# Weight checks loaded one output tile ahead, W2 casts spread over the first block, and three of seven W1 quadrants read without a copy

## What is computed

```python
tf = sigmoid(sum(cond, -1)); decay = exp(-exp(w)) * (0.5 + 0.5 * tf)
ek = exp(min(fside, 30)); ekv = ek * fside
# forward and backward scans over the 1024 time steps: a = a * decay + ekv_t ; b = b * decay + ek_t
num = nf + nb - ekv + exp(u + fside) * fside ; den = df + db - ek + exp(u + fside)
mixed = sigmoid(x) * num / max(den, 1e-8) * (0.8 + 0.2 * tf)
h = mixed @ W1.T                       # 1024 -> 4096
a = gelu(clip(round(h / 0.1)) * 0.1)
out = x + a @ W2.T                     # 4096 -> 1024
```

## Time and profile before

| | |
|---|---|
| median of 3 runs | 1911.16 us (1910.56 to 1913.1) |
| the profiled execution | 1906.45 us |
| its span in the profile | 1904.6 us |
| TensorE matmul busy | 1723.3 us, 90% |
| VectorE busy | 1281.7 us, 67% |
| ScalarE busy | 1046.7 us, 55% |
| last output matmul of block 0, 1, 7 ends at | 356.7, 576.9, 1897.6 us |

### The profile page before, as it was taken

One profiled execution on the slowest core, in us unless ns is written; L12 is line 12 of the kernel. 1 busy time (PEld: TensorE's weight loads), 2 busy tenths in 40 slices (PEclk: granted clock), 3 DMA queues, 4 the chain that ended last, 5 costly groups with the idle time before them and its releaser, 6 DMA issues.

```text
span 1904.6 us, 27493 instructions
## 1 busy us (share of the span) xinstructions
PE 1723.3 (90%) x10882; PEld 1076.1 (57%) x10882; DVE 1281.7 (67%) x2040; ACT 1046.7 (55%) x1422; POOL 24.7 (1%) x44
## 2 busy tenths in 40 slices
PE   1367989899998999899998999989998999989998
PEld 0123434487446864388545874478544884468643
DVE  8964987679586766678685775768776774933211
ACT  5544853488336863388444873378544883345400
POOL 0040000000000000000000000000000000000000
PEclk9678999899998999999998999989998999999999
DMA  8499866465454645456454654556454554545442
GB/s 215 116 238 334 299 204 182 144 198 191 148 168 143 188 150 177 144 181 213 139 174 136 199 170 142 171 169 194 153 183 132 178 189 148 157 132 161 142 146 73
DMA packets 119990, 329.55 MB, mean 173 GB/s; under 512 B 13232, under 2 KB 21424, under 8 KB 119344
## 3 DMA queue, kind: packets, MB, share of 16 engines
q1 hardware_dynamic: 117168, 304.67, 50.5%
q0 software_dynamic: 2688, 23.07, 5.1%
HBM read 319.30 MB, written 48.23 MB: 193 GB/s over the span
## 4 chain that ended last, share of the span: by engine, by line
PE 79%; DMA 3%; DVE 3%; ACT 1%; issue 1%; SPq 0%; DVEq 0%
PE ps L561 42%; PE ps L505 37%; DMA chk_full<-in_w_dram 3%; DVE chk_full L1107 1%; ACT chk_i L758 1%; DVE a L1039 0%; ACT mo L695 0%; DVE a L1041 0%; DVE a L1043 0%; DVE xy L1099 0%; SPq L303 0%; SPq L317 0%; DVE mo L1049 0%; SPq L318 0%; ACT q L699 0%
## 5 line engine op out<-in xcount | busy, mean ns | idle before, releaser
L561 PE MATMUL ps<-act,w_ring 128*128 128x512 f16 x4096 | 890.1, 379 | 9.4 <-DVE xy L1099 9.4
L505 PE MATMUL ps<-mo,w_ring 128*128 128x256 f16 x6272 | 704.4, 276 | 61.2 <-DVE mo L1049 59.6
L505 PEld LDWEIGHTS ps<-mo,w_ring 128*128 128x128 f16 x6272 | 620.5, 99 | 146.7 <-DVE mo L1049 61.6
L561 PEld LDWEIGHTS ps<-act,w_ring 128*128 128x128 f16 x4096 | 400.6, 98 | 490.9 <-issue 15.5
L758 ACT ACTIVATE chk_i<-chk_full 128x1024 int8<-128x1024 f32 x64 | 67.5, 1054 | 440.3 <-DMA chk_full<-in_w_dram 440.3
L1107 DVE SCALAR_TENSOR_TENSOR chk_full<-chk_i,chk_full 128x1024 f32<-128x1024 int8 x64 | 78.3, 1223 | 252.5 <-ACT chk_i L758 252.3
L1092 DVE SCALAR_TENSOR_TENSOR act<-a,act 128x1024 f16<-128x1024 f32 x128 | 156.2, 1220 | 132.3 <-ACT act L751 132.3
L745 ACT ACTIVATE a<-q 128x1024 f32<-128x1024 int16 x128 | 135.3, 1057 | 31.4 <-DVE act L1092 27.2
L751 ACT ACTIVATE act<-a 128x1024 f16<-128x1024 f32 x128 | 134.2, 1049 | 0.9
L482 PE MATMUL ps<-mo,w_ring 128*128 128x512 f16 x128 | 45.1, 532 | 87.3 <-DVE mo L1032 87.3
L495 PE MATMUL ps<-mo,w_ring 128*128 128x512 f16 x384 | 90.0, 399 | 16.5 <-ACT q L699 12.5
(11 more groups left out here) (95 smaller groups left out, 1454.2 us busy)
## 6 DMA issues: line engine op xcount, KB each, us to landing
w_ring<-w1s SPq DMA_DIRECT2D x168, 512.0 KB, 3.7
w_ring<-w_half SPq DMA_DIRECT2D x144, 512.0 KB, 4.2
chk_full<-in_w_dram SPq DMA_DIRECT2D x64, 512.0 KB, 5.2
V<-in_fside_dram SPq DMA_DIRECT2D x64, 256.0 KB, 4.5
R<-in_x_dram SPq DMA_DIRECT2D x64, 256.0 KB, 4.6
w_half<-in_w_dram POOLq DMA_DIRECT2D x16, 1024.0 KB, 14.5
xy<-in_x_dram SPq DMA_DIRECT2D x64, 256.0 KB, 2.6
out_dram<-xy SPq DMA_DIRECT2D x64, 256.0 KB, 4.4
```

The source lines that it names most:

```text
L505: mm = pe.matmul(dst[:, f, :], wp_ring[:, k, r, f, q, :], mo[:, op, q, p, :], start=(fresh and f == 0 and q == 0 and p == 0), stop=(q == K ...
L561: mm = pe.matmul(y_ps[y][:, :], w2_ring[:, k, f, :], act[:, a, p, :], start=(a == 0 and p == 0), stop=(a == FT - 1 and p == 1))
```

## The change

1. `load_check` moves ahead by one output tile: pieces 1 and 2 are asked for before the loop over d, and iteration d asks for piece d + 1. The wait inside it stays. One ring load moves between the two.
2. The hand-written order of DVE and ACT in the output stage is changed: the operands of group 0 and 1, parts of mixing tiles and the division of tile 7 now stand ahead of checks they stood behind.
3. The eight W2 casts no longer follow the W1 casts at once. Each waits on GpSimd for a point of the work: the seventh mixed tile, the first hidden steps, later hidden steps, the first outputs. The ring loads of W2 wait for the cast they need, not for all.
4. The 24 copies of plain W1 quadrants are gone. `w1s` holds the four sums only. The plain quadrants are read from `w1_half`, as two runs of 1 KB for each partition; a chunk of a plain and a summed quadrant is now loaded by two DMAs on one semaphore.

```diff
-        w1s = nc.dram_tensor("w1s", [STEPS, P, 7, 2, KH * P], F16).ap()
+        w1s = nc.dram_tensor("w1s", [STEPS, P, 4, 2, KH * P], F16).ap()
...
-                        yield flat[:, 0:2 * PROD], 2 * PROD, s_p5, g + 1
+                        yield [(0, PROD, w1_quads[s][:, 0, :, 0, :]), (PROD, PROD, flat[:, 0:PROD])], s_p5, g + 1
                         if s > 0:
-                            yield prev[:, 2 * PROD:4 * PROD], 2 * PROD, s_p3, g
-                        yield flat[:, 4 * PROD:6 * PROD], 2 * PROD, s_p6, g + 1
+                            prev = w1s[s - 1].rearrange("p r f q -> p (r f q)")
+                            yield [(0, 2 * PROD, prev[:, PROD:3 * PROD])], s_p3, g
+                        yield [(0, PROD, flat[:, 3 * PROD:4 * PROD]), (PROD, PROD, w1_quads[s][:, 0, :, 1, :])], s_p6, g + 1
                         if s > 0:
-                            yield prev[:, 6 * PROD:7 * PROD], PROD, s_p4, g
+                            yield [(0, PROD, w1_quads[s - 1][:, 1, :, 1, :])], s_p4, g
...
-                if i == 2 * STEPS:
-                    for d in range(DT):
-                        sp.wait_ge(s_w2cast[d], 16)
+                if 2 * STEPS <= i < 2 * STEPS + 4:
+                    sp.wait_ge(s_w2cast[i % 2], 16)
+                if 2 * STEPS + 4 <= i < 2 * STEPS + 2 * DT:
+                    sp.wait_ge(s_w2cast[(i - 2 * STEPS) // 2], 16)
...
-                for _ in range(3 if n == 0 else 5):
+                for _ in range(2 if n == 0 else 4):
                     ring_load()
                 load_check(DT * n + 1)
+                ring_load()
+                load_check(DT * n + 2)
                 for d in range(2, DT):
...
-                    load_check(DT * n + d)
+                    if d < DT - 1:
+                        load_check(DT * n + d + 1)
...
             for d in range(DT):
+                if d == 0:
+                    pool.wait_ge(s_out, CT - 1)
+                elif d == 1:
+                    pool.wait_ge(s_h0, 2 * FPS)
+                elif d < 6:
+                    pool.wait_ge(s_h0, FPS * (d + 3))
+                else:
+                    pool.wait_ge(s_y, d - 5)
                 pool.dma_start(w2_half[d], w2_full[d]).then_inc(s_w2cast[d], 16)
-            for s in range(STEPS):
-                pool.wait_ge(s_w1cast[s], 16)
-                for r, h, k in ((WP1, 0, 0), (WP2, 0, 1), (WP4, 1, 1)):
-                    pool.dma_start(w1s[s][:, r, :, :], w1_quads[s][:, h, :, k, :]).then_inc(s_w1copy, 16)
```

More of the change, by code:

```diff
@@ L262, in ring_chunks @@
                 w2_part = [[w2_half[d].rearrange("p (h n) -> p h n", h=2)[:, h, :] for h in range(2)] for d in range(DT)]
-                yield w2_part[0][0], SLOT, s_y, y_half(n, 0, 0)
+                yield [(0, SLOT, w2_part[0][0])], s_y, y_half(n, 0, 0)
                 if n > 0:
-                    yield last[:, 2 * PROD:4 * PROD], 2 * PROD, s_p3, g + 1
-                yield w2_part[1][0], SLOT, s_y, y_half(n, 1, 0)
+                    yield [(0, 2 * PROD, last[:, PROD:3 * PROD])], s_p3, g + 1
+                yield [(0, SLOT, w2_part[1][0])], s_y, y_half(n, 1, 0)
                 if n > 0:
-                    yield last[:, 6 * PROD:7 * PROD], PROD, s_p4, g + 1
-                yield w2_part[0][1], SLOT, s_y, y_half(n, 0, 1)
-                yield w2_part[1][1], SLOT, s_y, y_half(n, 1, 1)
+                    yield [(0, PROD, w1_quads[LAST][:, 1, :, 1, :])], s_p4, g + 1
+                yield [(0, SLOT, w2_part[0][1])], s_y, y_half(n, 0, 1)
+                yield [(0, SLOT, w2_part[1][1])], s_y, y_half(n, 1, 1)
                 for d in range(2, DT):
                     for h in range(2):
-                        yield w2_part[d][h], SLOT, s_y, y_half(n, d, h)
+                        yield [(0, SLOT, w2_part[d][h])], s_y, y_half(n, d, h)
         block = ctx.enter_context(nc.Block())
@@ L300, in ring_load @@
                 if i >= RING:
-                    sp.wait_ge(*chunks[i - RING][2:])
-                src, size = chunks[i][:2]
-                sp.dma_start(w_ring[:, i % RING, 0:size], src).then_inc(s_ring[i % RING], 16)
+                    sp.wait_ge(*chunks[i - RING][1:])
+                for place, size, src in chunks[i][0]:
+                    dst = w_ring[:, i % RING, place:place + size]
+                    if len(src.shape) == 3:
+                        dst = dst.rearrange("p (f q) -> p f q", f=2)
+                    sp.dma_start(dst, src).then_inc(s_ring[i % RING], 16)
             def load_prefix(g):
@@ L466, in _ @@
             used = [0]
+            pieces = [len(chunk[0]) for chunk in ring_chunks()]
             def loaded():
@@ L470, in loaded @@
                 used[0] = i + 1
-                pe.wait_ge(s_ring[i % RING], 16 * (i // RING + 1))
+                pe.wait_ge(s_ring[i % RING], 16 * sum(pieces[i % RING:i + 1:RING]))
                 return i % RING
@@ L840, in _ @@
                     reciprocal(g0 + 7)
-                check_i8(at + 7)
+                check_i8(at + 6)
                 if nxt:
                     operands_hi(n + 1, 3)
+                check_i8(at + 7)
             def general_block(m):
@@ L1180, in _ @@
                     operands_lo(n + 1, 0)
+                check(at)
                 residual_sum(n, 0)
-                check(at + 1)
+                if nxt:
+                    part(3, g0 + 4)
                 residual_sum(n, 1)
                 if nxt:
-                    part(3, g0 + 4)
                     part(0, g0 + 5)
-                check(at + 2)
+                check(at + 1)
                 if nxt:
@@ L1190, in _ @@
                     operands_lo(n + 1, 1)
+                    part(1, g0 + 5)
                 residual_sum(n, 2)
+                check(at + 2)
                 if nxt:
-                    part(1, g0 + 5)
                     part(2, g0 + 5)
                     part(3, g0 + 5)
-                check(at + 3)
                 residual_sum(n, 3)
@@ L1199, in _ @@
                     part(0, g0 + 6)
+                check(at + 3)
+                if nxt:
                     part(1, g0 + 6)
                     part(2, g0 + 6)
-                check(at + 4)
                 residual_sum(n, 4)
@@ L1206, in _ @@
                     part(0, g0 + 7)
+                check(at + 4)
+                if nxt:
                     part(1, g0 + 7)
-                check(at + 5)
                 residual_sum(n, 5)
@@ L1212, in _ @@
                     part(3, g0 + 7)
-                check(at + 6)
+                check(at + 5)
                 if nxt:
@@ L1216, in _ @@
                     operands_lo(n + 1, 2)
+                    divide(g0 + 7)
                 residual_sum(n, 6)
-                if nxt:
-                    divide(g0 + 7)
-                check(at + 7)
+                check(at + 6)
                 if nxt:
@@ L1223, in _ @@
                     operands_lo(n + 1, 3)
+                check(at + 7)
                 residual_sum(n, 7)
```

23 lines of the change are left out of this document (8 added, 15 removed).

## The result

| | before | after |
|---|---|---|
| median (lowest to highest) | 1911.55 us (1910.56 to 1913.1) | 1865.36 us (1860.87 to 1869.1) |
| the profiled execution | 1906.45 us | 1866.57 us |
| its span | 1904.6 us | 1864.0 us |
| last output matmul of block 0, 1, 7 ends at | 356.7, 576.9, 1897.6 us | 351.4, 566.3, 1857.0 us |

The kernel became faster, ratio 0.9757 (0.9733 to 0.9780), but by half of what was forecast: the two spans differ by 40.6 us, forecast were 90.5. It splits into 5.3 us by the end of block 0 (forecast 22 + 6.5) and 35.3 us in blocks 1 to 7 (forecast 59 + 3).

The account below looks back on a forecast made before the run. TensorE's full-rate work plus its stalls and half-clock time was taken as the bound. Gains of 59 + 3 + 22 + 6.5 = 90.5 us took the span from 1904.6 to 1814, hence a median of 1821 us, range 1802 to 1852.

Parts of the forecast that it names:

- 22 + 6.5: Block 0: 22 us gained in hidden steps 2 to 7, 6.5 us from an earlier residual sum 0.
- 59 + 3: Blocks 1 to 7: 59 us gained at the boundaries, 3 us from fewer L1099 pauses in the outputs' middle.
- Each cast has 20 us from its release to the ring load that waits for it: Block 0: 20 us allowed for each W2 cast to land, against a median of 14.5 us.
- 6.5 us, bounds 0 and 7: Block 0's outputs: gain from residual sum 0 at 242 us instead of 271.07, through DVE's lead.
- The walk: Step-by-step timing of an odd block's end under the new order, outputs ending at 576; trusted to about 2 us.
- Sum 4.0 to 4.3: Odd block's end: TensorE's pauses, 2.2 us for group 3's operand plus 1.8 for the seed, against 9.3 before.
- 0.4 + 1.8 + small = 2.5: Even block's end: TensorE's pauses total 2.5 us, as there is no prefix tile and DVE does 1.8 less.
- Pauses of 2 us are nearer the first, so I cost them at nothing: Block ends: a 0.84 us pause kept the clock, 8.6 halved it; short pauses cost 0, other end 2.4 a block.
- the boundary's 11.7: Old loss at each block end: 9.3 us of waiting plus 2.4 of cold clock, taken as all of a block's loss.
- The rival that starved the products: Product stage: 1 KB runs make the kernel slower, each stretch 21.5 us longer at four times the cost, 1971 us; chance 0.03.
- Boundaries stay half open: Rival for block ends: pauses of 5 to 6 us and a fallen clock, gain 28 not 59, 1852 us; chance 0.14.
- the start stays slow: Rival for block 0: its loads are themselves dense, gain 5 there, the rest as forecast, 1838 us; chance 0.10.

Follow-up runs that it names:

- four_casts: Changed kernel with W2 casts 4 to 7 left out, output tiles 4 to 7 using the weights of tiles 0 to 3; 1844.65 us, 0.9662.
- check_gpsimd_early: Changed kernel with check loads on GpSimd's queue and W2 casts 0 to 5 each behind a W1 cast in the mixing stage; 1796.26 us, 0.9413.
- runs_2kb: Changed kernel with plain quadrants read as one 2 KB run for each partition, other weights but the same bytes; 1861.97 us, 0.9750.
- ahead_only: Kernel before with only the check loads one tile ahead on SyncE and the new order of DVE and ACT; 1863.61 us, 0.9762.
- loads_back: Changed kernel with the check loads back at their old places on SyncE, everything else kept; 1860.36 us, 0.9757.
- before_check_gpsimd: Kernel before, with its old order, casts and copies, and only the 64 check loads moved to GpSimd's queue; 1825.98 us, 0.9571.
- even casts: Changed kernel with W2 casts 1 to 7 released one per hidden step, 13.8 us apart; 1856.68 us, 0.9728.
- check_gpsimd: Changed kernel with all 64 check loads on GpSimd's queue instead of SyncE's, each asked for when the check before is done; 1817.16 us, 0.9517.

## Why the prediction was wrong, and where it was right

Of the missing 49.9 us (90.5 - 40.6) 23.2 are block 0's and 26.7 the boundaries'.

**Start: the hidden layer was right, the casts' new price was missed.** The step that failed: "Each cast has 20 us from its release to the ring load that waits for it ... if one is late SyncE stands, but the ring holds 8 chunks." It weighs a cast only against the load that waits for this cast. But here a cast also delayed the other loads in flight (256 KB after 14.0 us) and SyncE's issues of them (two in 8.31 us, not 1.32), and the casts released at 201 to 229 us met the inputs of the last weight sums, in a stretch that the earlier trace rows showed at 87.7% even without them. four_casts (no late casts, no 12.8 us wait) and check_gpsimd_early (casts in the mixing stage, sums' inputs in 4.8 us, outputs with 0.48 us of wait) show it from both sides. The term "6.5 us, bounds 0 and 7" for residual sum 0 rested on DVE keeping its lead; the lower bound should have been a loss, since the measured term is -18.2 (118.1 to 136.3 us).

**Boundaries: the mechanism was right, its size was not.** The walk said that the wait in `load_check` would hold SyncE and with it the x loads: so it is. The term that failed is the pause at a block's end, "Sum 4.0 to 4.3" and, in an even block, "0.4 + 1.8 + small = 2.5". In block 1 residual sum 5 was late as walked and held no output, but it ran 16.7 us before the outputs' end (549.55 and 566.25) where the walk had 18.7 (557.3 and 576), and what follows it on DVE was later by about that. Residual sum 6 then stood 1.06 us more for its x: the walk had this sum ready by DVE's queue alone, and never asked when its x is loaded. The first product waits for it, 3.69 us. Pauses: 31.6 us, forecast 3 x 4.3 + 4 x 2.5 = 22.9, so 8.7 too few. Only 1.8 of them are in odd blocks (14.7, forecast 12.9). The even ones have 16.9 where 10.0 were forecast: at each of their ends TensorE waits 1.98 us for operands of group 3, which follow residual sum 6 and check 6, and the walk had 0.4 in all up to there.

**Clock: the other end came.** "Pauses of 2 us are nearer the first, so I cost them at nothing": the clock was 0.50 behind the ends of blocks 1 and 2 and 1.00 behind that of block 4, and what is left after the waits is 2.0 us a block, of the 2.4 named as the other end. In all it is 1505.6 - 7 x 208.6 - 31.6 = 13.8 us.

**Middle of the outputs: counted twice.** The 3.9 us for which 3 us of gain stood as a term of their own did go, since all waits of L568 are now in block 0. But the boundary's 11.7 was already more than a block's whole loss of 11.5: 3 us were promised twice, and 7 x 0.2 = 1.4 that were never lost. With 8.7, 13.8 and these 4.4 the sum comes to 26.9 of the 26.7 us missing.

**1 KB runs: right.** No cost that can be measured, by the change's queue (64.3%) and by runs_2kb. The rival that starved the products is out.

**What part did what** was not asked at all, and is what the runs answer best. ahead_only gives the whole gain, within the noise: the new casts and quadrants win 23.5 us in the hidden layer and lose 18.2 in the outputs. loads_back gives the whole gain too: the load ahead, the change's first part, is worth nothing beside the new order. And before_check_gpsimd gives 1.8 times the change's gain (0.0429 of the ratio against 0.0243) with the old order. In the kernel before the piece stood behind a ring load in SyncE's queue, in the changed one the x stands behind the piece: the queue was the cause both times.

**The rivals.** "Boundaries stay half open" (28 instead of 59 us) and "the start stays slow" (5 instead of 22) were given as alternatives, with 0.14 and 0.10. Both came about in size, for reasons that have nothing to do with each other: 1821 + 31 + 17 = 1869. That this is near the measured 1865 is in part luck: the pauses were 4.5 us, not 5 to 6, and the start's gain was not missing in the hidden layer, it was lost again in the outputs. Their being true together had no chance of its own, and so the range ended at 1852.

**What stays open.** Why pauses of 0.21 and 1.98 us halve the clock at the end of block 2, and 0.23 and 1.98 us do not at the end of block 6. Whether the new order of DVE and ACT alone gives the gain. And why the even casts gain less beside check_gpsimd (0.0010 of the ratio) than beside the change (0.0029); the intervals overlap, and the waits in block 0 that are left differ (8.49 and 4.35 us), but no run tells apart what else the queues carry then.

## What to carry to other kernels

A wait in a queue that works in order is paid by everything behind it: before a load is moved ahead, list what stands behind its wait, and ask whether an idle queue can hold it (64 loads moved to GpSimd's queue: 46 us). A transfer that is moved to be off one path must be weighed against all transfers of its new neighbourhood, not only against its own reader; put it where the DMA share is low and another engine sets the pace. And rivals that do not exclude each other need a chance for both.

## What the runs showed of the hardware that was not expected

- Nearly the same pauses of TensorE halve its clock at one place (0.50 behind 0.21 and 1.98 us) and not at another (1.00 behind 0.23 and 1.98 us).
- Loads of 256 KB beside four casts of 1024 KB landed after 14.0 us, without casts after 4.8 us, and two issues of them held SyncE for 8.31 us in place of 1.32; yet casts 0 to 5 in the mixing stage, at a DMA share of 0.88, cost nothing that shows (first products at 132.68 us, 132.21 in the change).
- Three of seven quadrants in runs of 1 KB: 8987 packets in place of 7022 in 80 us, share 64.3% against 61.9%, no time that can be measured.
